# Ten instead of eight of sixteen scan states summed by accumulating DMAs, the step size added by GpSimd, and a new timetable

## The reference, cut to what matters

```python
def step(h, inp):
    xt, dtt, bt, ct = inp
    dA = jnp.exp(A[None] * dtt[..., None])
    dB = dtt[..., None] * bt[:, None, :]
    h = dA * h + dB * xt[..., None]
    y = jnp.sum(h * ct[:, None, :], axis=-1)
    return (h, y)
...
x_ssm, z = jnp.split(x @ w_in.T + b_in, 2, axis=-1)
dt = jax.nn.softplus(x_ssm @ w_dt.T + b_dt)
y = (_selective_scan(x_ssm, dt, A, Bm, Cm) + D * x_ssm) * silu(z)
y = y @ w_out.T + b_out            # then layer norm, gate, feed-forward, gate
```

## Time and profile before

| | before |
|---|---|
| median of 3 runs | 4281.64 us (4272.67 to 4281.75) |
| the profiled execution | 4274.35 us, span 4272.6 us |
| mean granted TensorE clock | 0.983 of full speed |
| busy share of the span | PE 94%, ACT 89%, DVE 85%, POOL 81% |

### The profile page before, as it was taken

One profiled execution on the slowest core, in us unless ns is written; L12 is line 12 of the kernel. 1 busy time (PEld: TensorE's weight loads), 2 busy tenths in 40 slices (PEclk: granted clock), 3 DMA queues, 4 the chain that ended last, 5 costly groups with the idle time before them and its releaser, 6 DMA issues. The chain is left out here.

```text
span 4272.6 us, 68738 instructions
## 1 busy us (share of the span) xinstructions
PE 4033.6 (94%) x21664; PEld 2525.8 (59%) x21664; DVE 3646.4 (85%) x5134; ACT 3806.4 (89%) x6371; POOL 3460.0 (81%) x2058
## 2 busy tenths in 40 slices
PE   7889999999999999999999999999999999999987
PEld 3556666656666655666656656656666656666553
DVE  2788888988888988888988888988888888888884
ACT  3799999999999999999999999999999999999983
POOL 1788888888888888888888888888888888888882
PEclk8899999999999999999999999999999999999998
DMA  4677778787777787777788778787777787778773
GB/s 149 139 158 165 162 156 169 162 177 166 165 159 167 162 177 163 164 157 166 162 179 170 162 151 170 162 176 165 165 157 167 164 175 167 159 156 170 163 162 72
DMA packets 285535, 689.93 MB, mean 161 GB/s; under 512 B 31068, under 2 KB 33116, under 8 KB 285176
## 3 DMA queue, kind: packets, MB, share of 16 engines
q0 software_dynamic: 143360, 436.26, 56.0%
q1 hardware_dynamic: 141816, 249.29, 20.0%
HBM read 315.25 MB, written 101.74 MB: 98 GB/s over the span
## 5 line engine op out<-in xcount | busy, mean ns | idle before, releaser
L415 POOL TENSOR_TENSOR work<-work,c_bc 128x1024 f32<-128x1024 f32 x1024 | 2614.4, 2625 | 327.1 <-DVE work L1221 144.4
L1221 DVE TENSOR_TENSOR_SCAN work<-work,state,b_ps 128x512 f32<-128x512 f32 x1792 | 2235.9, 1272 | 183.7 <-PE b_ps L528 158.1
L926 ACT ACTIVATE work<-u_td,b_td 128x512 f32<-128x512 f32 x2048 | 1455.7, 711 | 180.8 <-DVE u_td L1306 90.6
L916 ACT ACTIVATE work<-dt_t,neg_a 128x512 f32<-128x512 f32 x2048 | 1453.9, 710 | 23.9 <-DVE work L1221 23.9
L528 PE MATMUL b_ps<-ident,work 128*128 128x128 f32 x8192 | 1214.3, 277 | 113.6 <-DVE work L1221 69.1
L528 PEld LDWEIGHTS b_ps<-ident,work 128*128 128x128 f32 x8192 | 960.1, 142 | 596.9 <-issue 261.3
L426 POOL DMA_DIRECT2D work<-work x512 | 477.5, 933 | 237.6 <-DMA work<-work 118.2
L603 PE MATMUL y_ps<-ident,work 128*128 128x128 f32 x4096 | 558.7, 276 | 20.1 <-DMA work<-work 19.9
L603 PEld LDWEIGHTS y_ps<-ident,work 128*128 128x128 f32 x4096 | 470.2, 141 | 171.2 <-issue 120.1
L677 PE MATMUL dense<-w_out_t,proj 128*128 128x512 f32 x1024 | 515.8, 606 | 0.0
L735 PE MATMUL dense<-xs_t,w_dt_t 128*128 128x512 f32 x1024 | 495.8, 593 | 0.0
(11 more groups left out here) (113 smaller groups left out, 3947.2 us busy)
## 6 DMA issues: line engine op xcount, KB each, us to landing
work<-work POOLq DMA_DIRECT2D x512, 512.0 KB, 5.5
c_bc<-c_d SPq DMA_DIRECT2D x512, 256.0 KB, 3.6
xn<-in_x SPq DMA_DIRECT2D x128, 256.0 KB, 5.2
dt_t<-tmp POOLq DMA_DIRECT2D x64, 512.0 KB, 5.1
work<-xs_t POOLq DMA_DIRECT2D x64, 512.0 KB, 6.3
xsh_d<-par_d SPq DMA_DIRECT2D x32, 1024.0 KB, 13.2
xsh_d<-in_x POOLq DMA_DIRECT2D x32, 1024.0 KB, 8.6
x<-xsh_d POOLq DMA_DIRECT2D x64, 512.0 KB, 7.0
```

Source lines behind the costliest of these rows:

```text
L415: gp.tensor_tensor(made_here, both(hs, HS_RING, s * U + i), c_bc[:, (s * N + n) % C_RING:(s * N + n) % C_RING + 1, :].to_broadcast([P, 2, ...
L916: A(decay[:, (s * U + i) % DEC_RING, :], dt_t[:, s % 2, j, :], ACT.Exp, scale=neg_a[:, j, n:n + 1]).then_inc(S["dec_done"], 1)
L926: A(v[:, n % V_RING, tb, :], u_td[:, tb, :], ACT.Copy, scale=b_td[:, s % 2, tb, n:n + 1]).then_inc(S["v_done"], 1)
L1221: V.tensor_tensor_scan(hs[:, (s * U + i) % HS_RING, :], decay[:, (s * U + i) % DEC_RING, :], b_ps[:, i % 2, :], state[:, i:i + 1] if s % N ...
```

## The change

- `HELD` gets states 12 and 13: ten states are summed by DMA, in five chains of three. State 15 stands alone. POOL issues 20 adding DMAs in a step instead of 16 (besides the two for the skip term), and PE adds 24 groups into `y_ps` instead of 32.
- The step size is added by four POOL instructions of 128x512 instead of two accumulating DMAs.
- `PE_AT` and `AT` are written anew.

```diff
-    HELD = (0, 1, 3, 4, 6, 7, 9, 10)
+    HELD = (0, 1, 3, 4, 6, 7, 9, 10, 12, 13)
...
-        dt_add=(49, 52),
-        u_mul=(54, 54, 56, 56),
+        dt_add=(44, 49, 51, 51),
+        u_mul=(49, 51, 52, 52),
...
-        y=(15, 18, 18, 18, 31, 31, 32, 34, 40, 42, 42, 42, 50, 50, 51, 52, 54, 55, 55, 56, 56, 57, 58, 58, 62, 63, 63, 63, 63, 64, 68, 68),
-        sum=(5, 8, 9, 11, 13, 16, 17, 20, 23, 25, 30, 31, 36, 37, 42, 44, 45, 48),
-        spread=19,
-        x_add=63,
+        y=(19, 19, 19, 19, 29, 30, 32, 34, 43, 44, 45, 45, 51, 51, 52, 54, 68, 68, 69, 70, 70, 70, 70, 70),
+        sum=(5, 7, 10, 12, 13, 16, 17, 22, 22, 26, 29, 34, 35, 37, 42, 43, 47, 47, 53, 57, 58, 62),
+        spread=35,
+        x_add=48,
...
-                for n in range(KD // 2):
-                    yield AT["dt_add"][n]
-                    gp.wait_ge(S["ldt_done"], at("ldt_done", f, 2 * n + 2))
-                    gp.dma_start(dt_t[:, f % 2, 2 * n:2 * n + 2, :], tmp[:, 2 * n:2 * n + 2, :], accum_op=ALU.add
-                                 ).then_inc(dt_added[n], Q)
+                for m in range(KD):
+                    yield AT["dt_add"][m]
+                    gp.wait_ge(S["ldt_done"], at("ldt_done", f, m + 1))
+                    gp.tensor_tensor(dt_t[:, f % 2, m, :], dt_t[:, f % 2, m, :], tmp[:, m, :], ALU.add
+                                     ).then_inc(S["dt_done"], 1)
```

More of the change, by code:

```diff
@@ L35, in build_program @@
     PE_AT = {}
[L36 to L45, removed]
+    for entry in """g.0@0 g.1@0 g.2@0 g.3@4 g.4@7 g.5@8 g.6@8 yz.0@8 g.7@8 res.0@8 yz.1@8 pre.0.0@8 yz.2@8 pre.0.1@9
+        yz.3@9 pre.0.2@10 out.0@10 pre.0.3@10 res.1@10 pre.1.0@12 out.1@12 pre.1.1@13 pre.1.2@14 out.2@17
+        pre.1.3@17 res.2@18 pre.2.0@18 out.3@18 pre.2.1@18 pre.2.2@19 pre.2.3@19 res.3@19 xt.0@20 pre.3.0@20
+        pre.3.1@21 pre.3.2@23 pre.3.3@23 z.0.0@25 xt.1@25 z.0.1@25 z.0.2@26 xt.2@26 z.0.3@26 xs.0.0@28
+        xt.3@28 xs.0.1@28 xs.0.2@29 xs.0.3@30 xs.1.0@31 xs.1.1@33 xs.1.2@34 xs.1.3@35 xs.2.0@36 xs.2.1@36
+        xs.2.2@37 xs.2.3@38 xs.3.0@38 xs.3.1@38 xs.3.2@38 xs.3.3@39 dt.0.0@40 dt.0.1@40 x2.0@42 dt.0.2@42
+        dt.0.3@42 dt.1.0@42 dt.1.1@42 x2.1@42 dt.1.2@44 dt.1.3@46 dt.2.0@46 dt.2.1@46 x2.2@47 dt.2.2@47
+        dt.2.3@49 dt.3.0@49 dt.3.1@49 x2.3@50 dt.3.2@50 dt.3.3@50 cb.0@50 cb.1@50 cb.2@51 cb.3@52 z.1.0@52
+        z.1.1@53 bt.0@53 z.1.2@54 z.1.3@54 z.2.0@55 ut.0@56 z.2.1@56 z.2.2@57 ut.1@57 z.2.3@57 s.0@58 ut.2@59
+        s.1@59 s.2@60 ut.3@61 s.3@61 z.3.0@62 z.3.1@62 z.3.2@63 z.3.3@63""".split():
         part, first = entry.split("@")
@@ L48, in build_program @@
     AT = dict(
[L49 to L52, removed]
-        dt_add=(49, 52),
-        u_mul=(54, 54, 56, 56),
[L55 to L58, removed]
+        store=(0, 9, 9, 14),
+        c_store=45,
+        x1=(18, 28),
+        bout=63,
+        dt_add=(44, 49, 51, 51),
+        u_mul=(49, 51, 52, 52),
+        gate=(40, 56, 59, 8),
+        relu=(62, 62, 0, 0, 0, 3, 6, 7),
@@ L59, in build_program @@
+        gm=7,
+        skip=(6, 10, 13, 13),
         rstdx=20,
         xn=(20, 20, 20, 20),
[L61 to L73, removed]
-        y_copy=(7, 7, 7, 7),
-        yz=(9, 10, 11, 13),
@@ L89, in build_program @@
-        x_add=63,
+        t2=(16, 19, 21, 24),
+        rstd2=38,
+        xn2=(38, 38, 38, 38),
+        h2=(40, 44, 47, 50),
+        h=(23, 25, 26, 28),
+        xs=(35, 37, 38, 39),
+        cb=52,
+        bt=52,
+        edt=(42, 48, 51, 51),
+        ldt=(42, 48, 51, 51),
+        ez=(36, 56, 60, 7),
+        lz=(36, 56, 60, 7),
+        sig=(36, 56, 60, 7),
+        y_copy=(7, 7, 7, 7),
+        yz=(7, 8, 9, 10),
+        out=(11, 15, 17, 18),
+        pre=(11, 17, 19, 24),
+        dt=(43, 47, 49, 51),
@@ L90, in build_program @@
+        ut=(57, 58, 60, 61),
+        z=(27, 55, 58, 63),
+        s=61,
+        stx=(3, 5, 16, 18),
+        nmrx=18,
+        st2=(25, 30, 36, 39),
+        nmr2=39,
+        y=(19, 19, 19, 19, 29, 30, 32, 34, 43, 44, 45, 45, 51, 51, 52, 54, 68, 68, 69, 70, 70, 70, 70, 70),
+        sum=(5, 7, 10, 12, 13, 16, 17, 22, 22, 26, 29, 34, 35, 37, 42, 43, 47, 47, 53, 57, 58, 62),
+        spread=35,
+        x_add=48,
     )
@@ L220, in build_program @@
         S = {n: ctx.enter_context(nc.semaphore(n)) for n in once + list(COUNT)}
[L221 removed]
+        x_loaded, c_loaded, wm_loaded, sum_done, skip_added, x1_added = (
             [ctx.enter_context(nc.semaphore(f"{n}_{m}")) for m in range(count)]
             for n, count in (("x_loaded", TB), ("c_loaded", C_RING), ("wm_loaded", 6), ("sum_done", KD // 2),
[L224 removed]
+                             ("skip_added", KD // 2), ("x1_added", TB // 2)))
         def at(name, k, n):
@@ L485, in inputs @@
                         gp.wait_ge(S["xs_done"], at("xs_done", f, KD))
-                    gp.wait_ge(dt_added[m // 2], (f + 1) * Q)
+                    gp.wait_ge(S["dt_done"], at("dt_done", f, m + 1))
                     gp.tensor_tensor(u_t[:, m, :], dt_t[:, f % 2, m, :], xs_t[:, m, :], ALU.mult
@@ L912, in decays @@
                     act.wait_ge(S["neg_done"], 2)
-                    act.wait_ge(dt_added[0], (s + 1) * Q)
-                    act.wait_ge(dt_added[1], (s + 1) * Q)
+                    act.wait_ge(S["dt_done"], at("dt_done", s, KD))
                 act.wait_ge(S["scan_done"], at("scan_done", s, i + 1 - DEC_RING))
@@ L941, in relu @@
                     act.wait_ge(S["s_copied"], at("s_copied", c, 1))
-                    act.wait_ge(dt_added[0], min(c + 3, NCH) * Q)
+                    act.wait_ge(S["dt_done"], at("dt_done", c + 2, 1))
                 elif j < RELU_RING:
@@ L1318, in take_z @@
                     if m:
-                        dve.wait_ge(dt_added[m // 2], min(f + 1, NCH) * Q)
+                        dve.wait_ge(S["dt_done"], at("dt_done", f, m + 1))
                     dve.wait_ge(S["t2_done"], at("t2_done", b, m + 1))
```

2 lines of the change are left out of this document (1 added, 1 removed).

## The result

The changed kernel takes 4355.11 us (median of 3 runs, 4350.48 to 4355.63) against 4281.64 before: ratio 1.018, 95% interval 1.0164 to 1.0195. It is slower, and it lies above the forecast range.

What follows compares the result with a forecast made beforehand. PE was taken to bound slots 48 to 63 and DVE slots 0 to 7, no engine the whole step. Terms -4.7 + 2.1 = -2.6 us a step, -83 over 32 steps, gave 4198 us from 4281.6; range 4115 to 4300.

Steps and rivals of the forecast that it cites:

- The two terms of the sum: Per step: +2.1 us in slots 0 to 47 and -4.7 us in slots 48 to 63, together -2.6 us.
- Slots 0 to 47: Larger of PE and DVE work over six stretches rises 89.5 to 90.9 us; with an added wait, +2.1 a step.
- the wait for `yz`: `yz` block 0 at slot 7 makes DVE wait for PE's turned-back block: 0.7 us taken, ends 0 and 1.5.
- the test of the count against the kernel before: Counted PE and DVE work per eight slots gave 77.4 us for slots 8 to 47, against 78.1 measured; therefore trusted.
- Slots 48 to 63: With the step size on POOL, these slots take 32.9 us instead of 37.6: -4.7 a step.
- POOL's prices: Slots 48 to 63: product 2.31 us, adding DMA 0.61 to issue or 1.25 behind its product, add or u 1.25.
- POOL from the end of scan 47: POOL's work list starts when scan 47 ends: u ready after 18.3 us, product of slots 52 and 53 after 20.6.
- the walk of POOL: POOL's list to 20.6 us, where DVE waits 2.2 at scan 58, then 12.3 of DVE work: 32.9 us.
- Adding DMAs: Four more in slots 53 to 62, hidden at DMA share 0.58; if not, slot 62's sum delays slot 5's `y_ps` groups.
- Rival 2: `spread` at slot 35 delays slot 37's sum; POOL late from 12.6 us landing; +1.8 a step, about 4340 us; chance 0.22.
- Rival 1: POOL's backlog is hidden: slots 48 to 63 take 30.7 us, the step 123.4, about 4130 us; chance 0.18.
- Rival 3: ACT holds PE: ACT's surplus in slots 0 to 7 half comes through, 1.5 us a step, 4246 us; chance 0.15.

Runs made afterwards that it cites:

- e10: e8 with POOL's four step-size additions on only 16 of 512 columns, the rest of that sum left out: 4207.51 us, 0.9853 of the kernel before.
- e1: Changed kernel with `spread` moved back from slot 35 to 19, nothing else: 4304.69 us, 1.0068 of the kernel before.
- e8: Changed kernel with `spread` back at slot 19, `x_add` at 63 and the four stores at 5, 10, 13, 18: 4249.26 us, 0.9917 of before.
- e2: Changed kernel with `x_add` (1 MB adding DMA) moved back from slot 48 to 63, nothing else: 4322.67 us, 1.0107 of the kernel before.
- e5: Changed kernel with `spread` back at slot 19 and `x_add` back at 63: 4259.05 us, 0.9953 of the kernel before.
- e9: e8 with the step size added by two DMAs (slots 49, 52), u at 54 to 55, `ut.0` at 57: 4415.61 us, 1.0337 of the kernel before.

## Why the prediction was wrong, point by point

**The two terms of the sum.** In e10, where both transfers and the stores are back, POOL is 0.1 us late at slot 47, and PE hardly waits for sums (14.5 us in all), slots 0 to 47 take 92.8 us against 90.5 before (+2.3, where +2.1 was forecast), and slots 48 to 63 take 33.4 against 37.7 (-4.3, -4.7 forecast). Both terms come near once those waits are gone, the second partly by luck (below); what the sum left out are the waits that the new timetable makes.

**Slots 0 to 47.** In the changed kernel they take 95.4 us, 4.9 more than before. Slots 40 to 47 were counted at 16.0 and took 17.7 with `spread` at 35, 16.2 with it back. Slots 0 to 7 were forecast at 15.2 with the wait for `yz` (0.7 taken; the trace has 0.75), and took 16.7; e10 gives 15.2. One count was off in both kernels: slots 16 to 23, 18.7 before and 16.4 with the change, measured 17.4 and 17.7. Slots 24 to 31 before were counted at 13.6 and took 15.2, so the test of the count against the kernel before, 77.4 for 78.1 over slots 8 to 47, held two errors that cancelled.

**Slots 48 to 63.** POOL's prices were right. From the start of the product of slots 46 and 47 to u it took 18.9 us (2169.4 - 2150.5; 18.3 forecast), to the end of the product of 52 and 53 21.2 (20.6). The step that failed is its starting point, "POOL from the end of scan 47": POOL starts 3.1 us late in this step, 2.9 in the mean, and 0.4 with `spread` put back (e1). The waits came where the text had put them, PE at `ut` and DVE at scan 58, and the two stretches took 35.7 instead of 32.9. In e10 PE is full in both stretches, by its windows of one step:

```profile
2077.64:2094.79 17.15, 17.15 (x111) 10.54 (x110) 14.42 (x18) 15.11 (x27) 15.00 (x13) 1.00 0.44 92
2094.79:2111.05 16.26, 16.26 (x81) 9.85 (x81) 15.43 (x23) 16.13 (x27) 15.74 (x11) 1.00 0.70 147
```

PE was counted at 15.6 and 14.7 here. The matmuls in these two windows, at the forecast's own prices, make some 32.5 us (an estimate from their count in the trace): a group of `dt.2`, entered at slot 47, and work of the next step run here as well. e8, with additions of full length, takes the same 33.4 us with PE full, and its u is ready 18.4 us after scan 47, as the walk had it (18.3). So even a POOL that is on time leaves 33.4 us, and the 32.9 came near it by luck: PE is the bound there, not the walk of POOL that gave the number.

**Adding DMAs.** "They are hidden there" fell. A share of 0.58 of the DMA engines over a stretch says nothing of a transfer of 1 MB that starts just before the sum; the condition named behind it (the sum of slot 62 delays the groups of slot 5) came true (2.85 us in the row of PE above).

**Rival 2** had the mechanism and nearly the time (4340), for more reasons than it named. Its landing of 11.1 us at slot 37 is below the 12.6 from which it was to decide; it decided since POOL was 3.1 us late at slot 47 where "landing less 10" gives 1.1. Its net price, measured by e1, is 50 us. `x_add` at slot 48, moved too, was costed as 0.8 us of POOL and nothing else: with e2 it is 32 us. **Rival 1**, POOL's backlog hidden, forecast 123.4 a step; e10 comes nearest to its condition and takes 126.2, since PE then fills slots 48 to 63. The granted clock of 0.93 in slots 0 to 7 that it hoped to raise was that of one step; over 24 steps it is 0.98 before and 0.98 with the change. **Rival 3** did not show: PE's waits for ACT's inputs fell (38.7 us before, 30.8 with the change), and DVE's for the decays rose only from 0.8 to 9.6 us in all.

**The clock.** The sum has no term for it, and it moves some of these numbers. In slots 16 to 23 of the changed kernel sixteen of the 24 steps have a granted clock of 1.00 and take 17.2 us; eight have less and take 18.8. Before, all 24 have 1.00 there. In each kernel, steps with a lowered clock can be compared with the others in the same stretch; their surplus is 0.8 us a step in the change, 2.0 in e1, 1.6 in e2, 0.4 in e8 and e10 and next to nothing before. This is at most the clock's share, since the waits of those steps can be longer too, and no run held the two apart. So a part of the misses is the clock, and the gains of e1 and e2 are what is left after it.

Of the loss against the forecast (131.1 - 125.6 = 5.5 us a step), 3.1 go with the two transfers (e5), 1.1 more by the profiled executions with the stores (0.3 by the medians), 0.7 to 1.3 with the length of the additions (e10); 126.2 is left. The clock's share is contained in these parts.

The Trainium skill, "DMA: Bandwidth & Descriptors", section "Issuing engines are not separate DMA queues", states that transfers of all engines interleave on the same 16 DMA engines. The runs agree: a sum lands after 5.8 us in the median, and after 11.1 where it was issued beside `spread`, which SP issued.

## What to carry to other kernels

When a timetable moves a large transfer, walk through every small transfer that is in flight beside it, and ask which engine stands in line for its landing and how much slack that engine has there; a mean DMA share does not answer this. Cost a list of work from where its engine will be, not from the event that could start it. A wait can cost more than its length: behind PE's wait in e9 the clock was at half for 4.3 us. Parts of a change can depend on each other: here neither half was worth anything in the old timetable, and with two entries put back (e5) the whole is 0.5% faster than before, with the stores too (e8) 0.8%.
